# First attention group's stacks from selection products on TensorE, V copies on GpSimd, and last stores from two queues, in a fused attention and FFN kernel

## What is computed

```python
def attn(x):                       # B, S, D = 8, 1024, 256
    qkv = x.reshape(B, S, H, hd).transpose(0, 2, 1, 3)     # 16 heads, hd = 16
    w = einsum('bhqd,bhkd->bhqk', qkv, qkv) / sqrt(hd)
    w = softmax(where(causal, w, min))
    return einsum('bhqk,bhkd->bhqd', w, qkv) ...
def ffn(x, W1, b1, W2, b2, scale):
    lt = x[:, 1:17];  even, odd = lt[:, ::2], lt[:, 1::2]
    m1 = (even[:, :4, :, None] * odd[:, :4, None, :]).reshape(B, 1024, 256)
    m2 = (even[:, 4:, :, None] * odd[:, 4:, None, :]).reshape(B, 256, 1024)
    h = einsum('bsd,hd->bsh', x, W1) + scale * einsum('bsd,bhd->bsh', x, m1) + b1
    h = gelu(h)
    return einsum('bsh,oh->bso', h, W2) + scale * einsum('bsh,boh->bso', h, m2) + b2
xn = layernorm(x);  out = x + attn(xn) + ffn(xn, ...)
```

## Time and profile before

| | us |
|---|---|
| median of 3 runs (875.97 to 876.32) | 875.99 |
| the profiled execution | 876.32 |
| its span in the trace | 874.5 |
| PE busy in the span | 843.8 (96%) |
| ACT busy | 695.7 (80%) |
| DVE busy | 661.3 (76%) |
| POOL busy | 255.1 (29%) |

### The profile page before, as it was taken

One profiled execution on the slowest core, in us unless ns is written; L12 is line 12 of the kernel. 1 busy time (PEld: TensorE's weight loads), 2 busy tenths in 40 slices (PEclk: granted clock), 3 DMA queues, 4 the chain that ended last, 5 costly groups with the idle time before them and its releaser, 6 DMA issues.

```text
span 874.5 us, 16279 instructions
## 1 busy us (share of the span) xinstructions
PE 843.8 (96%) x6288; PEld 432.5 (49%) x6288; DVE 661.3 (76%) x1344; ACT 695.7 (80%) x751; POOL 255.1 (29%) x520
## 2 busy tenths in 40 slices
PE   3699999999999999999999999999999999999997
PEld 3353645546454464545545464454645446454453
DVE  6786697957978599776997679896797858973252
ACT  3678788887888878888788878888788887888874
POOL 1213244132422314133241323413143231422311
PEclk9699999999999999999999999999999999999999
DMA  5968257590756617374274924749075661712202
GB/s 170 244 153 161 84 165 179 77 207 5 190 157 97 182 73 168 110 152 127 86 167 116 166 95 154 170 90 191 25 192 158 93 186 71 162 23 53 57 1 37
DMA packets 187148, 109.16 MB, mean 125 GB/s; under 512 B 139016, under 2 KB 155456, under 8 KB 186176
## 3 DMA queue, kind: packets, MB, share of 16 engines
q1 hardware_dynamic: 185344, 106.52, 51.2%
q10 hardware_dynamic: 1728, 1.61, 0.6%
HBM read 74.49 MB, written 33.61 MB: 124 GB/s over the span
## 4 chain that ended last, share of the span: by engine, by line
PE 93%; ACT 2%; DVE 2%; DMA 2%; issue 0%; ACTq 0%; SPq 0%; DVEq 0%
PE o_ps L519 31%; PE work L550 22%; PE work L534 21%; PE scores L499 18%; ACT probs L419 2%; PE work L561 1%; DMA k_stack<-k_dram 1%; DMA q_dram<-xt_pair 1%; DVE xn L641 0%; DMA xn<-x 0%; DVE stats L622 0%; DVE o_sb L738 0%; DVE newton L636 0%; DVE newton L635 0%; PE work L569 0%
## 5 line engine op out<-in xcount | busy, mean ns | idle before, releaser
L419 ACT ACTIVATE probs<-scores 128x1024 f32<-128x1024 f32 x576 | 558.1, 1023 | 106.2 <-PE scores L499 106.1
L411 POOL TENSOR_SCALAR_AFFINE_SELECT probs<-probs 128x256 f32<-128x256 f32 x512 | 252.6, 514 | 608.1 <-ACT probs L419 600.5
L519 PE MATMUL o_ps<-probs,v_ones 128*32 128x512 f32 (+3 forms) x3072 | 279.8, 493 | 0.5 <-DVE o_sb L738 0.5
L499 PE MATMUL scores<-q_stack,k_stack 64*128 64x512 f16 (+3 forms) x1536 | 187.3, 330 | 12.0 <-DMA k_stack<-k_dram 8.7
L519 PEld LDWEIGHTS o_ps<-probs,v_ones 128*32 128x32 f32 x3072 | 83.7, 109 | 129.1 <-issue 113.8
L499 PEld LDWEIGHTS scores<-q_stack,k_stack 64*128 64x128 f16 x1536 | 52.9, 94 | 172.6 <-ACT probs L419 105.9
L550 PE MATMUL work<-g_hi,w_hi 128*128 128x512 f32 x256 | 112.9, 441 | 0.0
L534 PE MATMUL work<-xt_hi,w_hi 128*128 128x512 f32 x256 | 103.2, 403 | 0.0
L550 PE MATMUL work<-g_hi,w_lo 128*128 128x512 f32 x256 | 102.6, 401 | 0.0
L550 PE MATMUL work<-g_lo,w_hi 128*128 128x512 f32 x256 | 101.1, 395 | 0.0
L534 PE MATMUL work<-xt_hi,w_lo 128*128 128x512 f32 x256 | 99.9, 390 | 0.0
(11 more groups left out here) (57 smaller groups left out, 635.9 us busy)
## 6 DMA issues: line engine op xcount, KB each, us to landing
q_stack<-q_dram SPq DMA_DIRECT2D x63, 256.0 KB, 4.0
k_stack<-k_dram SPq DMA_DIRECT2D x126, 128.0 KB, 4.0
q_dram<-xt_pair SPq DMA_DIRECT2D x31, 512.0 KB, 4.9
w<-w1t SPq DMA_DIRECT2D x8, 1024.0 KB, 7.5
k_dram<-xt_pair SPq DMA_DIRECT2D x16, 512.0 KB, 3.3
xt_w<-w2t SPq DMA_DIRECT2D x8, 1024.0 KB, 6.5
acc<-x SPq DMA_DIRECT2D x32, 256.0 KB, 6.2
out<-acc SPq DMA_DIRECT2D x128, 64.0 KB, 2.9
```

The lines of the kernel that those rows point to most:

```text
L411: pool.affine_select(out=blk, in_=blk, compare_op=ALU.is_ge, fill=0.0, base=0, pattern=[[0, 2], [1, P]], channel_multiplier=-1).then_inc(m ...
L419: act.activation(probs[:, slot % RING, 2 * half:2 * half + 2, :].rearrange("p h q -> p (h q)"), scores[:, half, :], ACT.Exp, scale=EXP_SCA ...
L499: last = pe.matmul(scores[:, half, h * BANK + at:h * BANK + at + n], k_stack[rows, g % 2, half, kb * P:(kb + 1) * P], q_stack[rows, g % 2, ...
L519: last = pe.matmul(o_ps[VW * j:VW * (j + 1), half, q0 % BANK:q0 % BANK + n], v_ones[:, kb, heads_of(g).start + 2 * j, :], probs[:, slot % ...
```

## The change

- **Stacks of group 0 for tokens 0 to 511.** POOL makes eight 0/1 matrices (sel, fp16, in the space of q_stack for group 1). PE multiplies them with xt_pair (8 matmuls of 512 columns in the scores banks), which spreads the heads' rows as the stacks want them. ACT copies the k half to k_stack, DVE the q half to q_stack. Slot 0 waits for these two copies (first_stacks). The DMAs for group 0's stacks now bring tokens 512 to 1023 alone, all six from SP's queue, and slot 2 waits for them.
- **xt.** ACT copies the two banks of features 0 to 127, DVE those of 128 to 255 (first_xt_late).
- **Even rows.** Their products go through the two work banks of FFN, four rows at a time, between the scores of slots 0 and 1, and ACT's copies stand behind the exps of slots 0 and 1. FFN's first block waits for both copies.
- **V copies** of batch 0 go from ACT to POOL, ahead of its masks.
- **SP** waits for first_stacks ahead of group 1's stacks and for first_rows ahead of batch 1's x.
- **Last stores.** Of the last four DMAs of the output SP issues two and ACT two.

```diff
 # SP
-        def stacks_half(eng, b, g, h):
+        def stacks_half(eng, b, g, h, tok=slice(0, S)):
...
             sp.wait_ge(pair_out[0], 16 * STORE_DMAS)
-            stacks_half(sp, 0, 0, 0)
+            for h in range(2):
+                stacks_half(sp, 0, 0, h, slice(BANK, S))
             sp.wait_ge(xt_split, 1)
             load_w2()
             store_heads(0, 1)
+            sp.wait_ge(first_stacks, 2)
             load_stacks(0, 1)
             load_acc(0)
...
                     sp.wait_ge(v_ready, GROUPS * (b + 1))
+                    if b == 0:
+                        sp.wait_ge(first_rows, 2)
                     load_x(b + 1)
...
-                for j in range(QUARTERS):
+                for j in range(QUARTERS // 2 if (b, half, t) == (B - 1, 1, 1) else QUARTERS):
+                    out_quarter(sp, b, half, t, j)
 # GpSimd
+            pool.memset(sel, 0.0).then_inc(sel_zero, 1)
+            pool.wait_ge(sel_zero, 1)
+            pool.wait_ge(ident_made, 1)
+            for k in range(2):
+                for u in range(GH // 2):
+                    one = ident[:, :][:, HEAD_ROWS * u:HEAD_ROWS * (u + 1)].rearrange("p (h g c) -> p h g c", h=2, g=2)[:, :, 0, :]
+                    for part in range(2):
+                        rows = sel[:, k, u, part, :].rearrange("p (h c a e) -> p h c a e", h=2, c=HD, a=2)
+                        rows = rows[:, :, :, :, part] if k else rows[:, :, :, part, :]
+                        ins = pool.tensor_copy(rows, one.unsqueeze(3).broadcast_to([P, 2, HD, 2]))
+            ins.then_inc(sel_made, 1)
+            pool.wait_ge(xn_ready, 1)
+            for g in range(GROUPS):
+                pool.tensor_copy(v_ones[:, :, heads_of(g), 0:HD],
+                                 xn[:, :, :].rearrange("p t (h d) -> p t h d", h=HEADS)[:, :, heads_of(g), :])\
+                    .then_inc(v_ready, 1)
 # ACT
             q_part(act, 0, 0, 1)
-            for u in range(XT_USES):
+            act.wait_ge(spread, 1)
+            act.copy(k_stack[:, 0, :, 0:BANK], scores[:, 0, :].rearrange("p (u s) -> p u s", u=2)).then_inc(first_stacks, 1)
+            for u in range(2):
                 act.wait_ge(first_lo, u + 1)
-                act.copy(xt[:, u // 2, BANK * (u % 2):BANK * (u % 2 + 1)], first_bank[u]).then_inc(first_xt, 1)
+                act.copy(xt[:, 0, BANK * u:BANK * (u + 1)], first_bank[u]).then_inc(first_xt, 1)
+            exps(0)
             copy_even(0)
-            act.wait_ge(pair_out[0], 16 * STORE_DMAS)
-            stacks_half(act, 0, 0, 1)
+            exps(1)
             copy_even(1)
-            act.wait_ge(v_ones_made, 1)
-            for g in range(GROUPS):
-                copy_v(g)
-            exps(0)
-            exps(1)
...
+            act.wait_ge(o_added, 2 * GROUPS * B)
+            act.wait_ge(ffn_added, 2 * DT * B)
+            for j in range(QUARTERS // 2, QUARTERS):
+                out_quarter(act, B - 1, 1, 1, j)
 # PE
-                if i == 0:
+                if slot == 0:
+                    pe.wait_ge(first_stacks, 2)
+                elif slot == 2:
+                    pe.wait_ge(stacks_in[0], 16 * STACK_DMAS)
+                elif i == 0:
...
                     pe.wait_ge(xt_split, b + 1)
+                    if b == 0:
+                        pe.wait_ge(first_even, 2)
...
-            for i in range(2 * NLORA):
...
-            pe.wait_ge(first_even, 2)
+            pe.wait_ge(sel_made, 1)
+            pe.wait_ge(first_lo, 1)
+            for k in range(2):
+                for u in range(GH // 2):
+                    for part in range(2):
+                        last = pe.matmul(scores[:, k, BANK * u:BANK * (u + 1)], sel[:, k, u, part, :],
+                                         xt_pair[:, part, 0, 0:BANK], start=part == 0, stop=part == 1)
+                last.then_inc(spread, 1)
+            def spread_even(half):
+                for i in range(NLORA):
+                    row = 2 * (NLORA * half + i) + 1
+                    last = pe.matmul(work[:, i // 2, D * (i % 2):D * (i % 2 + 1)], ...)
+                last.then_inc(first_rows, 1)
             scores_of(0)
+            pe.wait_ge(first_xt, 2)
+            spread_even(0)
             scores_of(1)
+            pe.wait_ge(first_even, 1)
+            spread_even(1)
...
-                        pe.wait_ge(first_xt, XT_USES)
+                        pe.wait_ge(first_xt_late, 2)
 # DVE
             dve.wait_ge(consts_in, 16 * (1 + QUARTERS))
-            dve.wait_ge(first_xt, XT_USES)
+            dve.wait_ge(spread, 2)
+            dve.tensor_copy(q_stack[:, 0, :, 0:BANK], scores[:, 1, :].rearrange("p (u s) -> p u s", u=2))\
+               .then_inc(first_stacks, 1)
+            for u in range(2):
+                dve.tensor_copy(xt[:, 1, BANK * u:BANK * (u + 1)], first_bank[2 + u]).then_inc(first_xt_late, 1)
+            dve.wait_ge(first_xt_late, 2)
+            dve.wait_ge(first_xt, 2)
             scale_odd()
             split_xt()
             add_m1(0)
```

More of the change, by code:

```diff
@@ L254, in attention_ffn @@
         first_rows, first_even = sem("first_rows"), sem("first_even")
+        first_xt_late, first_stacks = sem("first_xt_late"), sem("first_stacks")
+        sel_zero, sel_made, spread = sem("sel_zero"), sem("sel_made"), sem("spread")
         pair_out = [sem(f"pair_out{t}") for t in range(DT)]
@@ L266, in attention_ffn @@
         block = ctx.enter_context(nc.Block())
+        sel = q_stack[:, 1, :, :].rearrange("p u s -> p (u s)")[:, 0:8 * P].rearrange("p (k u a m) -> p k u a m", k=2, u=2, a=2)
         first_bank = [work[:, 0, :], work[:, 1, :], o_ps[:, 0, :], o_ps[:, 1, :]]
@@ L277, in acc_quarter, with out_quarter @@
                           x[b, :, :].rearrange("(a r) (t j c) -> j r t a c", r=VW, t=DT, j=QUARTERS)[j]).then_inc(acc_in[b % 2], 16)
+        def out_quarter(eng, b, half, t, j):
+            rows = slice(BANK // VW * half, BANK // VW * (half + 1))
+            eng.dma_start(out[b, :, :].rearrange("(a r) (t j c) -> j r t a c", r=VW, t=DT, j=QUARTERS)[j, :, t, rows, :],
+                          acc[VW * j:VW * (j + 1), b % 2, t, rows, :]).then_inc(out_stored, 16)
         def q_part(eng, b, t, part):
@@ L282, in q_part @@
                           xt_pair[:, part, t, :].unsqueeze(1).broadcast_to([P, 2, S])).then_inc(pair_out[t], 16)
-        def stacks_half(eng, b, g, h):
+        def stacks_half(eng, b, g, h, tok=slice(0, S)):
             rows = slice(HEAD_ROWS * h, HEAD_ROWS * (h + 1))
-            eng.dma_start(q_stack[rows, g % 2, :, :],
-                          q_dram[b, heads_of(g), :, :, :, :].rearrange("(u h) c a e s -> h (c a e) u s", h=2)[h])\
+            n = tok.stop - tok.start
+            eng.dma_start(q_stack[rows, g % 2, :, tok],
+                          q_dram[b, heads_of(g), :, :, :, tok].rearrange("(u h) c a e s -> h (c a e) u s", h=2)[h])\
                .then_inc(stacks_in[g % 2], 16)
             for u in range(GH // 2):
-                eng.dma_start(k_stack[rows, g % 2, u, :],
-                              k_dram[b, heads_of(g), :, :, :].rearrange("(u h) c a s -> u h (c a) s", h=2)[u, h]
-                              .unsqueeze(1).broadcast_to([2 * HD, 2, S])).then_inc(stacks_in[g % 2], 16)
+                eng.dma_start(k_stack[rows, g % 2, u, tok],
+                              k_dram[b, heads_of(g), :, :, tok].rearrange("(u h) c a s -> u h (c a) s", h=2)[u, h]
+                              .unsqueeze(1).broadcast_to([2 * HD, 2, n])).then_inc(stacks_in[g % 2], 16)
         @block.sync
@@ L307, in store_acc @@
                 sp.wait_ge(ffn_added, 2 * DT * b + DT * half + t + 1)
-                rows = slice(BANK // VW * half, BANK // VW * (half + 1))
-                for j in range(QUARTERS):
-                    sp.dma_start(out[b, :, :].rearrange("(a r) (t j c) -> j r t a c", r=VW, t=DT, j=QUARTERS)[j, :, t, rows, :],
-                                 acc[VW * j:VW * (j + 1), b % 2, t, rows, :]).then_inc(out_stored, 16)
+                for j in range(QUARTERS // 2 if (b, half, t) == (B - 1, 1, 1) else QUARTERS):
+                    out_quarter(sp, b, half, t, j)
             def load_w1():
@@ L420, in exps @@
                                    scores[:, half, :], ACT.Exp, scale=EXP_SCALE).then_inc(exp_done, 1)
-            def copy_v(g):
-                act.copy(v_ones[:, :, heads_of(g), 0:HD],
-                         xn[:, :, :].rearrange("p t (h d) -> p t h d", h=HEADS)[:, :, heads_of(g), :]).then_inc(v_ready, 1)
             def copy_even(half):
                 act.wait_ge(first_rows, half + 1)
-                act.copy(even[:, NLORA * half:NLORA * (half + 1), :].rearrange("p i d -> p (i d)"), scores[:, half, :])\
+                act.copy(even[:, NLORA * half:NLORA * (half + 1), :].rearrange("p i d -> p (i d)"),
+                         work[:, :, :].rearrange("p a n -> p (a n)"))\
                    .then_inc(first_even, 1)
@@ L571, in _ @@
                 last.then_inc(first_t, 1)
```

(12 more changed lines are left out.)

## The result

| | median us | span of the profiled execution |
|---|---|---|
| before | 875.96 | 874.5 |
| changed | 879.09 | 877.2 |

The ratio is 1.0036, with a 95% interval of 1.0026 to 1.0046: the changed kernel is slower by 3.1 us, and its time lies above the predicted range of 874.2 to 878.0.

What follows compares the result with a forecast made beforehand. It took DVE's chain to its first FFN copy, not PE's stack path, to bound the start. Block 2 -1.2, clock +2.15 and tail -0.45 gave +0.5 us: 876.5 against the median of 875.99, range 874.2 to 878.0.

Steps and rivals of the forecast that it cites:

- What bounds: Start of batch 0: PE's path through the stacks is slack; DVE's nearly as long chain to its first copy sets FFN's block 2.
- The term -1.2 for block 2: FFN's first layer, batch 0: DVE's first copy frees bank 0 at 39.8, 1.2 us before the 41.03 of now.
- The wait and copies ahead of scale_odd: DVE, start: 1.0 us wait for the spread plus 2.07 us of copies; scale_odd at about 20.7, 1.7 us late.
- split_xt, add_m1 and split_m1 take 11.41 us: DVE, behind scale_odd: this stretch keeps its 11.41 us and ends at 32.1.
- the moved masks at 20.8 us: GpSimd, behind the V copies: masks start not before the first exp ends at 20.8; slow V copies would delay them.
- Clock, +2.15: PE, FFN's blocks 2 and on: after waiting for DVE, a 4.3 us stretch at half clock loses 2.15 us.
- Tail, -0.45: Last four stores: two issuing queues let the DMA engines pack without gaps, 0.45 us less, between 0 and 0.97.
- the 0.97 us: Last four stores: upper end of the tail's gain, with the 1.94 us of issue halved by two queues.
- W2: W2's load, start: issued at 25.6, lands at 32.1, so DVE waits no longer; the high end costs 2.1 us.
- The sum: Whole kernel: start -1.2 + 2.15 = +0.95, tail -0.45, together +0.5 us; 876.5 against the median.
- The "slower" rival: Start: W2 lands at 34.2, bank 0 is free 0.9 us later than now; +2.6 us, 878.6; chance 0.11.

Runs made afterwards that it cites:

- both edits: Changed kernel, with gelus straight from the banks in batch 0's first chunk and xt copies ahead of the wait for the spread products: 871.53 us, 0.9951 of before.

## Why the prediction was wrong

By its own steps:

- **What bounds: right.** The path through the stacks was slack behind DVE's chain, and PE waited 2.79 us for DVE's copy ahead of block 2. The run with direct gelus on the changed kernel, which takes this wait away and 5.4 us of span with it, shows it.
- **The term -1.2 for block 2: wrong, and the step that failed.** I had it at 39.8; it came at 42.12, +1.09 us against before. Two parts of DVE's chain were mis-sized. The wait and copies ahead of scale_odd put it at 21.36 and not 20.7 (my own terms, 17.50 + 1.0 + 2.07, add to 20.57). The spread came 0.4 us later than taken: its eight products took 2.86 us, not 2.5, although the granted clock of 15.9 to 18.8 is 1.00, where my price for full clock was 1.9; why is open. And the q_stack copy has 1024 elements (two halves of 512) and takes 1.23 us where I had counted the 0.69 of 512. The larger part was "split_xt, add_m1 and split_m1 take 11.41 us": they took 13.3. I had placed the moved masks at 20.8 us and asked who would wait for them, but not what runs beside them in their new place. The run with small masks shows 1.9 us for ten masks, the one with 16 selects 2.65 for these. The Trainium skill ("GPSIMD Engine Reference", Key points) says that GpSimd shares its SBUF interfaces with VectorE and contends with VectorE's instructions in a two-port mode or with two SBUF inputs. The rows agree in the main: the differences of the splits, with two SBUF inputs, were stretched (2.50 to 3.34 us for four), while the low parts that DVE made from PSUM beside GpSimd's V copies kept their 0.69 us. Stretched were also the splits' casts, with one input (1.43 to 1.85 for four); no row shows in which mode they run. And add_m2, with inputs like add_m1's, took 4.89 us beside four masks in the kernel before and 4.75 without masks in the changed one; why it pays so little, no run shows.
- **Clock, +2.15: right in kind, 0.6 too high.** It fell twice; the first fall lay under DVE's work, and the second cost 1.55 us. I had taken a cold stretch of 4.3 us; here it lasted 3.1 (42.12 to 45.2). In the run with small masks it lasted 4.4 us (40.24 to 44.6), and the loss was 2.23.
- **Tail, -0.45: wrong.** It was -0.07 in the changed kernel and nothing by itself. A share of 0.79 was not room to fill: with two queues the share rose and the bytes per second stayed. The Trainium skill ("DMA: Bandwidth & Descriptors", Issuing engines are not separate DMA queues) says that issuing from several engines saves only the time of the issue. The trace agrees: the issue was shorter by 1.0 us. But the issue was not what ended last, so the 0.97 us that the prediction drew from this did not come either.
- **W2: nearly right, and that DVE did not wait was luck.** Issued at 26.25, it landed 6.3 us later, at about 32.5, where I had 32.1. DVE did not wait for it in the changed kernel because DVE was 2.5 us late itself; in the run with small masks it waited 0.18 us.
- **The sum.** +1.09 + 1.55 - 0.07 = +2.6 us, and 2.7 in the span (3.1 between the medians), where I had -1.2 + 2.15 - 0.45 = +0.5. The "slower" rival had W2 late at the same place and so came near the time (878.6), with the wrong cause. Without the masks' 1.9 us the mechanism came out much as forecast: in the run with small masks block 2 starts 0.79 us sooner than before, the clock takes back 2.23, and the time, 877.14, lies inside the predicted range.

## What to carry to other kernels

When a wait is cut, look for the second path that ends beside it: here DVE's first FFN copy followed an idle time of only 0.5 us, so it could have freed the bank at 40.0 at the soonest, 1.0 us ahead of block 2, and the 7.8 us won on PE (38.2 to 30.4) could buy no more than that one. Of work that moves in time, ask not only who waits for it but also what runs beside it in its new place; a mask on GpSimd that was nearly free beside one operation (add_m2) cost DVE 0.2 us beside others (the splits and add_m1). And a wait of PE, here of 2.3 to 4.6 us, may bring a half-speed stretch behind it, which has to be counted too; some matmuls into a free bank can be cheaper than that stretch.

## What was not expected

- A 256-element select on GpSimd beside DVE's splits and add_m1 slows both engines: 0.41 to 0.61 us for the select, and 0.17 to 0.19 us more for DVE. With 4 elements in the select DVE lost nothing.
- The clock's fall in the same place differs from one run to the next: a wait of 2.3 us for W1 went by at full clock in the profiled run of both edits, and the same wait of 2.3 us was followed by half clock in the run with the copies turned round. One of 3.8 us ended at half with direct gelus, and at the end of the kernel before the clock fell 2.0 us after the last matmul.
- The last 256 KB, in rows of 128 bytes, move at 120 to 122 GB/s from one queue and from two.
